# Layer 0 of a graph network: three gathering passes replaced by one pass that builds two dense matrices, and three dense passes

## The reference, cut to what matters

```python
def L0(y, edge_index, edge_weight):            # 3 steps of propagation
    norm = deg_inv_sqrt[row] * edge_weight * deg_inv_sqrt[col]
    out = y
    for _ in range(3):
        agg = segment_sum(norm[:, None] * out[row], col, num_segments=6250)
        out = clip(agg * 0.9 + 0.1 * y, 0.0, 1.0)
    return out

def L1(n_feat, e_feat, ...):                   # 6 steps; once before them:
    eh = relu(e_feat @ en1_w.T + en1_b)        # [200000, 128]
    ...
# L2 (graph convolution) and L3 (self loops) sum rows over the same edges, unweighted,
# but for self edges, which L2 counts and L3 leaves out.
```

## Time and profile before

| | |
|---|---|
| median of 3 runs | 32663.71 us |
| profiled execution | 32413.36 us |
| its span (first to last instruction) | 32411.6 us |
| mean granted TensorE clock | 0.686 |
| busy in the span | PE 56%, DVE 37%, ACT 20%, POOL 48% |
| layer 0, from scaled state to its layer norm | 3334.0 to 11999.4 us |
| two dense passes at the end | 31425 to 31881, 31913 to 32358 us |

### The profile page before, as it was taken

How to read it: one execution, slowest core, us unless ns; L and a number is a source line. 1 busy time by engine, 2 the same in 40 slices (tenths; PEclk the granted TensorE clock), 3 DMA queues, 4 the chain that set the end, 5 groups by cost and what they waited for, 6 DMA issues and landing times. The chain is left out here.

```text
span 32411.6 us, 403512 instructions
## 1 busy us (share of the span) xinstructions
PE 18026.4 (56%) x104961; PEld 13157.7 (41%) x104961; DVE 11934.9 (37%) x35567; ACT 6546.6 (20%) x20858; POOL 15499.2 (48%) x15719
## 2 busy tenths in 40 slices
PE   3334332333344447665766576667666766676654
PEld 3333221221211125544554455445544554455444
DVE  5443222222477754332333233323332333233320
ACT  0000111111111113222322232223222322232210
POOL 5884466456444544453445344534453445344520
PEclk5555555655555558777877787778777877787777
DMA  3223121111122112221221122212221222122137
GB/s 95 49 49 86 47 56 46 52 54 50 45 80 69 49 32 70 63 56 48 70 63 56 49 70 62 56 49 69 62 57 49 69 62 56 51 69 62 56 114 317
DMA packets 1256771, 2157.89 MB, mean 67 GB/s; under 512 B 744415, under 2 KB 1032120, under 8 KB 1116522
## 3 DMA queue, kind: packets, MB, share of 16 engines
q10 hardware_dynamic: 423840, 1341.95, 12.1%
q0 software_dynamic: 502784, 263.58, 5.7%
q1 hardware_dynamic: 329576, 546.81, 4.9%
HBM read 1721.40 MB, written 761.91 MB: 77 GB/s over the span
## 5 line engine op out<-in xcount | busy, mean ns | idle before, releaser
L772 POOL DMA_INDIRECT sb_xg<-node_rows,sb_src_c x14112 | 13388.5, 949 | 14651.7 <-SPq L790 8683.5
L908 PE MATMUL banks<-sb_work,sb_eh_sb 128*128 128x256 f32 x29184 | 8441.9, 446 | 1103.5 <-issue 818.4
L861 DVE TENSOR_TENSOR sb_work<-sb_xs,banks_p 128x2048 f32<-128x2048 f32 x1824 | 4170.8, 2288 | 9736.7 <-remote 7067.5
L908 PEld LDWEIGHTS banks<-sb_work,sb_eh_sb 128*128 128x128 f32 x29184 | 6400.2, 226 | 2796.2 <-issue 1360.2
L965 ACT ACTIVATE sb_work<-banks 128x512 f32<-128x512 f32 x7296 | 4133.6, 599 | 11173.8 <-remote 7697.2
L894 PE MATMUL banks_p<-sb_work,sb_en 128*32 128x256 f32 x29184 | 2207.2, 394 | 1024.0 <-issue 1008.2
L851 DVE COPY sb_xs<-sb_xg 128x32 f32 x14592 | 1769.5, 193 | 2391.2 <-issue 2228.5
L365 POOL DMA_INDIRECT slots<-sb_rows,sb_slot_u x1600 | 2108.2, 1318 | 785.3 <-issue 756.9
L935 PE MATMUL banks_s<-sb_fold,sb_pj 128*128 128x32 f32 x1824 | 421.6, 305 | 3391.1 <-ACT sb_pj L977 2913.2
L1370 PE MATMUL banks<-sb_hot_code,sb_hot_row 128*128 128x392 bf16 x2432 | 1170.5, 506 | 1816.8 <-DVE sb_hot_code L1318 1330.6
L1155 PE MATMUL banks_s<-sb_fold,sb_s 128*128 128x32 f32 x608 | 192.0, 409 | 3251.3 <-DVE sb_s L1094 2989.6
(11 more groups left out here) (284 smaller groups left out, 14777.9 us busy)
## 6 DMA issues: line engine op xcount, KB each, us to landing
sb_eh_sb<-eh ACTq DMA_DIRECT2D x912, 1024.0 KB
adjacency<-sb_work ACTq DMA_DIRECT2D x153, 3136.0 KB
sb_work<-adjacency SPq DMA_DIRECT2D x98, 3136.0 KB, 12.3
sb_xg<-node_rows,sb_src_c POOLq DMA_INDIRECT x14112
eh<-sb_eh_sb ACTq DMA_DIRECT2D x304, 512.0 KB
sb_win_row<-window_rows SPq DMA_DIRECT2D x100, 488.3 KB
slots<-sb_zeros SPq DMA_DIRECT2D x19, 2368.0 KB
sb_rowin<-slots SPq DMA_DIRECT2D x152, 296.0 KB, 3.2
```

What stands on the lines that cost most here:

```text
L772: nc.gpsimd.indirect_dma_start(m.xg_ring[:, row % RING * D:(row % RING + 1) * D], None, m.node_dram, bass.IndirectOffsetOnAxis(ap=m.src_c[ ...
L861: V.tensor_tensor(m.spread[q], m.xs[h].rearrange("s (t i) -> s t i", i=D)[:, tiles, :].unsqueeze(3) .broadcast_to([P, TS, D, WN]), m.mask_ ...
L908: o = mm(m.ps_pair[u % 4][:, v, :, :], m.eh[h % 2][:, t * K:(t + 1) * K], m.spread[t // TS][:, t % TS, :, :], start=True, stop=True)
```

## The change

The three calls of `plain_pass` and `adjacency_pass`, each followed by `add_tiles`, are gone. `build_cells` runs once, ahead of the first step, and gathers nothing. Per tile it makes two tables side by side, of weights and of counts (784 columns, one instruction of VectorE over two half-size tables, `CELLS` = 49 x 64). The one-hot of codes stays on VectorE. GpSimd makes four one-hots of rows of 128 x 128 per tile: one plain one, with self edges left out, and three that hold a weight's high, middle and low part in bfloat16. TensorE multiplies the three into one accumulated product and the plain one into the other: four matmuls of 392 columns in place of one. PSUM holds two such pairs. A slot is now 8 windows, so that its two tables are as large as one was (2 x 1568 KB); there are 98, and the flush is asked for every half batch. The same pass encodes the edge features, half a batch at a time, into one buffer. Each step is then a `dense_pass` over the weights, without own rows.

```diff
-        if encode is not None:
-            plain_pass(nc, m, 1, m.fold, encode)
-        else:
-            adjacency_pass(nc, m)
-        add_tiles(nc, m)
+        dense_pass(nc, m, 0, None, m.fold)
...
+    build_cells(nc, m)
     scaled_state(m.x)
-    step(0)
-    step(1)
-    for _ in range(2, STEPS0):
-        step(None)
+    for _ in range(STEPS0):
+        step()
```

`build_cells`, engine by engine (its first phase is that of `adjacency_pass`):

```diff
+        @block.sync
+            for i, n, h in batches(sp):
+                for q in range(2):
+                    if not first(i, h):
+                        sp.wait_ge(turned, 2 * n + q - 1)
...
+                    sp.dma_start(m.attr[q].rearrange("s (t f) -> s t f", f=D),
+                                 slots_v[:, bass.ds(n * TC + q * EC, EC), META:ROW]).then_inc(rows_in[q], 16)
+        @block.gpsimd
...
+                G.tensor_copy(pair(own_code), halves(F16)[:, :, 4:6]).then_inc(ready, 1)
+                G.tensor_copy(pair(own_weight), halves(BF16)[:, :, 2:4]).then_inc(ready, 1)
+                G.tensor_copy(own_low, m.low[:, bass.ds(n * TC, TC)]).then_inc(ready, 1)
...
+                G.tensor_scalar(m.row_now[h % 2], rows, float(P), -float(P), ALU.is_ge, ALU.mult).then_inc(ready, 1)
...
+                G.tensor_tensor(m.row_now[h % 2], m.row_now[h % 2], rows, ALU.add).then_inc(ready, 1)
...
+                for t in range(TC):
+                    if t % HOTS == 0 and not (first(i, h) and t < 2 * HOTS):
+                        pool.wait_ge(tabled, n * TC + t - HOTS)
...
+                    G.tensor_scalar(m.hot_row[0][:, t % (2 * HOTS), :], m.codes[:, 0:P], own_code[:, 2 * t + 1:2 * t + 2], None,
+                                    ALU.is_equal)
+                    for k, w in enumerate((own_weight[:, 2 * t:2 * t + 1], own_weight[:, 2 * t + 1:2 * t + 2],
+                                           own_low[:, t:t + 1])):
+                        r = G.tensor_scalar(m.hot_row[1 + k][:, t % (2 * HOTS), :], m.codes[:, 0:P], m.row_now[h % 2][:, t:t + 1], w,
+                                            ALU.is_equal, ALU.mult)
+                    r.then_inc(rows_hot, 1)
+        @block.scalar
...
+                act.wait_ge(added, b * TS)
+                for k in range(2):
+                    act.dma_start(m.cells_dram[k][bass.ds(row, P), :], m.cells[:, bass.ds(third + k * CELLS, CELLS)],
+                                  cond=done).then_inc(flushed[g % 2], 16)
+            def rectify(c):
+                act.wait_ge(biased, c + 1)
+                nc.scalar.activation(m.eh_now, m.eh_now, ACT.Relu).then_inc(relu, 1)
+                act.wait_ge(relu, c + 1)
+                act.dma_start(m.eh_dram[:, bass.ds(c * EC * K, EC * K)], m.eh_now).then_inc(eh_out, 16)
+            for i, n, h in batches(act):
+                for q in range(2):
+                    c = n * 2 + q
...
+                    nc.scalar.activation(m.attr_t[q], m.ps_turn[q], ACT.Copy).then_inc(turned_sb, 1)
+                    if not (first(i, h) and q == 0):
+                        rectify(c - 1)
+                        flush(i, c, 2 * h + q)
+        @block.vector
...
+                    V.tensor_scalar(m.hot_code[t % HOTS], m.codes[:, :], m.code[h % 2][:, 2 * t:2 * t + 1], None,
+                                    ALU.is_equal).then_inc(codes_hot, 1)
...
+                    V.scalar_tensor_tensor(here, here, m.keep[:, bass.ds(n * TC + t, 1)], m.ps_both[t % 2],
                                            ALU.mult, ALU.add).then_inc(added, 1)
...
                 for t in range(TC):
+                    q = t // TS
+                    if t % TS == 0 and not first(i, h):
+                        dve.wait_ge(flushed[1 - q], 32 * n)
                     if t + ahead < TC:
                         name(t + ahead)
                     add(t)
+                    if t % TS == TS // 2 and not (first(i, h) and q == 0):
+                        bias(n * 2 + q - 1, first(i, h) and q == 1)
+        @block.tensor
...
+                    for g in range(2):
+                        mt = nc.tensor.transpose(m.ps_turn[q][:, g * P:(g + 1) * P], m.attr[q][:, g * P:(g + 1) * P],
+                                                 m.ident[:, :])
...
+                    for t in range(q * TS, q * TS + TS):
+                        pe.wait_ge(rows_hot, n * TC + t + 1)
+                        pe.wait_ge(codes_hot, n * TC + t + 1)
+                        if not (first(i, h) and t < 2):
+                            pe.wait_ge(added, n * TC + t - 1)
...
+                        for k in range(3):
+                            mm(m.ps_cells[t % 2][0], m.hot_row[1 + k][:, t % (2 * HOTS), :], code,
+                               start=(k == 0), stop=(k == 2))
+                        mm(m.ps_cells[t % 2][1], m.hot_row[0][:, t % (2 * HOTS), :], code, start=True,
+                           stop=True).then_inc(tabled, 1)
...
+                    for g in range(2):
+                        me = mm(m.ps_encoded[:, g, :], m.attr_t[q][:, g * P:(g + 1) * P], m.en1[:, :], start=True, stop=True)
```

`dense_pass` takes the matrix and loads a slot as two blocks of 128 rows; without own rows it skips their load, VectorE's copies and the matmul of L1420:

```diff
-                sp.dma_start(m.slot_cells[h], m.cells_dram[bass.ds(n * P, P), :]).then_inc(slot_in[h], 16)
+                sp.dma_start(m.slot_cells[h], m.cells_dram[matrix][bass.ds(n * 2 * P, 2 * P), :]
+                             .rearrange("(g p) c -> p g c", p=P)).then_inc(slot_in[h], 16)
```

`name_cells` keeps codes for half batches and slots of 8 windows, raises the row code of a self edge by 128, so that the plain one-hot misses it (GpSimd takes the 128 off again for the weights' rows), and splits each weight in three (some eight more instructions over all 2432 tiles):

```diff
+            step(V.tensor_copy(high, meta[:, :, 1]))
+            step(V.tensor_tensor(m.cell[:, :], meta[:, :, 1], high, ALU.subtract))
+            step(V.tensor_copy(middle, m.cell[:, :]))
+            step(V.tensor_tensor(m.low[:, :], m.cell[:, :], middle, ALU.subtract))
+            step(V.tensor_copy(weight[:, :, 2], high))
+            step(V.tensor_copy(weight[:, :, 3], middle))
```

More of the change, by code:

```diff
@@ L1230, in _, with flush @@
         @block.scalar
         def _(act):
-            def flush(i, b, h):
-                table = bass.at_runtime_partition(m.flush_at[0:1, 3 * h:3 * h + 3], i)
+            def flush(i, b, g):
+                table = bass.at_runtime_partition(m.flush_at[0:1, 3 * g:3 * g + 3], i)
                 _, (third, row, done) = nc.values_load_multi_w_load_instructions(
-                    table, engines=[mybir.EngineType.Activation], min_val=0, max_val=SLOTS * P,
-                    skip_runtime_bounds_check_because="name_cells keeps the third below THIRDS * CELLS and the row below (SLOTS + 1) * P")
-                act.wait_ge(added, b * TC)
-                act.dma_start(m.cells_dram[bass.ds(row, P), :], m.cells[:, bass.ds(third, CELLS)],
-                              cond=done).then_inc(flushed[h % 2], 16)
@@ L1283, in _ @@
-            for h in range(L):
-                act.wait_ge(stored[h], BODIES * 16)
+                    table, engines=[mybir.EngineType.Activation], min_val=0, max_val=(THIRDS - 1) * 2 * CELLS,
+                    skip_runtime_bounds_check_because="name_cells keeps the third below THIRDS * 2 * CELLS and the row at 2 * SLOTS * P or below")
+                act.wait_ge(added, b * TS)
+                for k in range(2):
+                    act.dma_start(m.cells_dram[k][bass.ds(row, P), :], m.cells[:, bass.ds(third + k * CELLS, CELLS)],
+                                  cond=done).then_inc(flushed[g % 2], 16)
@@ L1286, in _ @@
+            rectify(2 * BATCHES - 1)
+            flush(BODIES, 2 * BATCHES, 0)
+            act.wait_ge(flushed[1], 32 * BATCHES)
+            for k in range(2):
+                act.dma_start(m.cells_dram[k][0:P, :], m.cells[:, k * CELLS:(k + 1) * CELLS]).then_inc(flushed[1], 16)
+            act.wait_ge(flushed[0], 32 * BATCHES)
+            act.wait_ge(flushed[1], 32 * BATCHES + 32)
+            act.wait_ge(eh_out, 32 * BATCHES)
         @block.vector
@@ L1310, in add_cells @@
-                V.tensor_copy(m.code[h % 2].rearrange("s (t k) -> s t k", k=2), codes[:, :, 4:6]).then_inc(coded, 1)
-                dve.wait_ge(coded, n + 1)
+                dve.wait_ge(ready, n * 5 + 1)
                 def name(t):
-                    if t >= HOTS:
+                    if not (first(i, h) and t < HOTS):
                         dve.wait_ge(tabled, n * TC + t - HOTS + 1)
-                    V.tensor_scalar(m.hot_row[t % HOTS], m.codes[:, 0:P], m.code[h % 2][:, 2 * t + 1:2 * t + 2], None,
-                                    ALU.is_equal).then_inc(hot, 1)
@@ L1380, in dense_pass @@
         slot_in = (slot_a, slot_b)
+        loaded = 16 if own_dram is None else 32
         def by_slot(eng):
```

416 lines of the change are left out of this document (118 added, 298 removed).

## The result

The changed kernel took 32762.62 us (median of 9 runs, 32736.91 to 32778.9), the kernel before beside it 32664.95 (9 runs): a ratio of 1.0028, 95% interval 1.0018 to 1.0039. It is slower by about 0.3%, where 6.5% faster was forecast. The profiled execution has a span of 32760.7 us at a clock of 0.705 (before 0.686).

The account below looks back on a forecast made before the run. Layer 0 as a chain of phases, its counting pass a VectorE loop; 8665 us removed, 1424 fixed and 5110 for build_cells (304 halves of 16.8 us) added, net -2131: 30530 us, range 29250 to 32000.

Parts of the forecast that it names:

- GpSimd's half batch: GpSimd's eight tiles in build_cells: 32 operations at 0.43 us, 13.8, plus 1.0 small ones and 1.5 port: 16.3 us.
- The prediction's estimate of 0.25 to 0.3 us: Price of one GpSimd operation by the Trainium skill; with it the sum would be that of the first rival, 29920 us.
- The break-even: Half batch of build_cells from which the change is slower: 23.8 us, reached by a GpSimd operation of 0.67 us.
- that rival: Slower than before: the port adds VectorE's and GpSimd's times in build_cells, 28.7 us a half, 34150 us; chance 0.11.
- its side remark: A GpSimd operation of 0.67 us reaches the 23.8 us half batch without any port.
- the third rival: GpSimd is dear: 0.55 to 0.65 us an operation, 20 to 23 us a half, 31500 to 32420 us; chance 0.14.
- The port: Port pair shared by VectorE and GpSimd in build_cells: 1.6 us a half charged to VectorE, 1.5 to GpSimd.
- The stand: VectorE waiting for the flush at the head of a half in build_cells: 7.7 us, 97 times, 750 us.
- The rival "TensorE is the bound": TensorE at 1.2 GHz bounds build_cells: 17.1 us and gaps, 18 a half, 30890 us; chance 0.13.
- the 15.5 given to VectorE: VectorE's half batch in build_cells: 13.0 us with the port, plus 2.5 on average for the flush, 15.5 us.
- Layer 1: The layer after layer 0, not touched by the change: to stay at 19.4 ms within 0.5%.

Follow-up runs that it names:

- dve_all: Changed kernel with all four one-hots of rows made by VectorE, GpSimd keeping five small instructions a batch: 25181.13 us, ratio 1.0200.
- split_two_again: split_two run again on a chip of the slower kind, with the flush still behind the rectifier: 30814.67 us, ratio 0.9439.
- split_two: Changed kernel with VectorE making the plain and high one-hots, GpSimd the middle and low: 24355.93 us on chip 8, ratio 0.9865.
- split_two_ff: split_two with ScalarE's flush sent ahead of the rectifier of the same half: 30228.27 us, ratio 0.9242.
- act_scale: Changed kernel with GpSimd making two plain compares a tile, ScalarE scaling one by three weight parts, flush ahead of rectifier: 30052.35 us, ratio 0.9190.
- before_b: Kernel before, unchanged, run again for a trace; its theory A: chips differ in how soon gathered rows land. 32699.74 us, on the slower kind of chip.

## Why the prediction was wrong

**The step that failed is GpSimd's half batch:** "I take twice the iota's line, 0.43". Measured 0.59 and 0.79 us, at a pitch of 0.58 and 0.78. Eight tiles of 2.91 are 23.3 us, and with the small instructions (1.48 us a batch) 24.0 a half, near the build's 7370.8 / 304 = 24.2, where 13.8 + 1.0 + 1.5 = 16.3 stood. The prediction's estimate of 0.25 to 0.3 us, worked out from what the Trainium skill (GPSIMD Engine Reference, Performance versus the Vector engine) has for a good one-input loop, is not borne out by this case either: the compare costs 591 ns alone, and the measurement decides. (The tens of cycles of dispatch in it stand in the section Instruction dispatch of the same page.)

**The miss is this one term.** 304 x (24.25 - 16.8) = 2265 us. The other parts, from the trace after: name_cells 19.5 us longer (20 forecast); start of build_cells 29.4 (29.7); from there to VectorE's first add 6.3, and from its last to the scaled state 19.2 (neither forecast); scaled state and three steps 12165.3 - 10779.2 = 1386.1 (1374). Together +37. What was removed is 12053.6 - 3334 = 8720 in the second profile of the kernel before, whose execution took 32672 us, not the 8665 of an execution 0.8% below the median: -54. 2265 + 37 - 54 = 2248; the median missed the forecast by 32762.6 - 30533 = 2230. The 18 us between are within the scatter of what follows layer 0.

**The break-even was right and underweighted.** The text gave 23.8 us a half, and "an operation of GpSimd of 0.67 us reaches that without any port". That 0.67 is not without the port: it has the 1.5 us charged for it; without them it is (23.8 - 1.0) / 32 = 0.71. The mean of the four is (0.58 + 3 x 0.78) / 4 = 0.73, and the time came out just slower. The bounds were 0.22 and 0.949, so 0.67 lay inside them with much room above; yet the case had 0.11, named after the port. The mechanism of that rival was wrong, its side remark was the case; the mechanism of the third rival, "GpSimd is dear" (0.14), was right, but it ended at 0.65 us. The forecast leaned on the iota, which reads nothing and computes one value; the compare's slope is three times its 0.846 ns a column, with the multiply four times.

**The port.** Charged 1.6 us a half to VectorE and 1.5 to GpSimd. Against their shortest durations, naming lost (371 - 308) x 8 = 0.5 us and GpSimd's four (7221.8 - 7140.4) / 304 = 0.27. That the two engines delay each other shows all the same: naming lasted up to 817 ns beside a full GpSimd, and never over 342 in dve_all, where GpSimd is busy for 146 of 6257 us.

**The flush.** The stand was put at 7.7 us, 97 times, 750 us; split_two_again has 97 times, 685.2. It was right for a VectorE-bound build and off the path in this one (85 times, 295.3 us, and no time back when it goes). Its cause was partly mis-sized: between the issue of eh and the flush lie 2.3 us, not none.

**VectorE and TensorE.** The add lasts 1.03 (1.0 forecast), naming 0.31 at its shortest. TensorE's 392 columns at the lower level take (1.16 - 0.53) / 2 = 0.32 us each (0.33 forecast), but a granted clock of 0.63 went with an engine that waits; where GpSimd was relieved it rose, 0.84 in split_two, 0.88 in split_two_ff, 0.90 in act_scale. The rival "TensorE is the bound" found no support: TensorE waits 3006.7 us for GpSimd, and with a faster feed its granted clock was higher. split_two_ff has 15.8 us a half and 30228 us, near the 15.5 given to VectorE and near the forecast, but that is chance: there VectorE names three one-hots a tile instead of one and no longer stands for the stores. No run had a GpSimd of the assumed price, so the rest of the sum is checked term by term and not as a whole.

**Layer 1** was to stay within 0.5%; from the layer norm to the end the pair differs by 0.2%, within the scatter.

## What to carry to other kernels

Price an engine's operation by a row of the same kind before moving work to it; where the trace has none, take the chance of a loss rather from the share of the bounds' interval beyond the break-even, here (0.949 - 0.67) / (0.949 - 0.22) = 0.38, than from that of a story, here 0.11. Here moving one-hots from VectorE (0.25 to 0.31 us) to GpSimd (0.59 to 0.79) made an idle engine the bound; two of the four on each engine with the flush ahead give 0.924, two plain ones on GpSimd with the scaling on ScalarE 0.919. Work that looks late, such as the flush, is worth moving only when the engine that waits for it is the bound: 626 us in split_two, 7364.1 - 7356.0 = 8 us in the changed kernel.

## What the runs showed of the hardware

There are two kinds of chip here for this kernel. On chip 8 the kernel before takes 24685 us, on the others 32650 to 32700. split_two ran on both: its build is the same (5438.7 and 5418.3 us), but from the first layer norm on it lasts 14133 and 20580 us. Three lines of the gathering layer, first on chip 13, then on chip 8 (busy us, mean ns | idle before and its main releaser):

```profile
L785 POOL DMA_INDIRECT sb_xg<-node_rows,sb_src_c x9408 | 8876.4, 943 | 11907.8 <-SPq L803 6641.2
L921 PE MATMUL banks<-sb_work,sb_eh_sb 128*128 128x256 f32 x29184 | 8801.4, 452 | 1737.3 <-issue 1437.3
...
L864 DVE COPY sb_xs<-sb_xg 128x32 f32 x14592 | 1758.0, 190 | 2434.7 <-issue 2237.4
```

```profile
L785 POOL DMA_INDIRECT sb_xg<-node_rows,sb_src_c x9408 | 8899.6, 946 | 5467.6 <-issue 3700.1
L921 PE MATMUL banks<-sb_work,sb_eh_sb 128*128 128x256 f32 x29184 | 7672.5, 422 | 147.6 <-DVE sb_work L874 145.3
...
L864 DVE COPY sb_xs<-sb_xg 128x32 f32 x14592 | 1767.5, 209 | 4004.8 <-SPq L800 2654.0
```

Both issue the same 9408 gathers, of 944 ns each as medians. On the slower kind GpSimd waits 6641.2 us instead of 302.4 for SyncE's word (L803) that the ring has room, given when rows have landed and older ones are copied. By the waits it is not the landing that holds the layer up, as before_b's theory A had it: VectorE's copies (L864) wait 2654.0 us for the word that rows have landed (L800) on chip 8 and only 178.2 on chip 13. What the slower kind has more of is pauses of TensorE in its large matmuls (L921), 1437.3 us where the profile shows nothing that it waited for; the clock from the layer norm to the end was 0.76 there and 0.87 on chip 8. That points to the copying, behind a slower TensorE, as what is late; why TensorE pauses is open. The same pattern is in the kernel before on chip 11 (L908, 1315.9 us of such pauses).

The ratio of 1.0653 on chip 8 would follow if the removed passes were shorter there, as the build is not. If what follows layer 0 takes the kernel before 14133 us there as well, its layer 0 ends near 10550 us instead of 12054. No trace of the kernel before came from that chip, so this stays an inference.
